# Cross attention: the normalised probabilities split into two f16 parts in SBUF and turned by one transposing DMA a chunk, the keys by another, and an f32 product with the fused output weights

## The reference, cut to what matters

```python
# image_embeds = ctx_1024, latents = layernorm(x after layer 0)
x = layer_norm(image_embeds, ln1_g, ln1_b)
l = layer_norm(latents, ln2_g, ln2_b)
q = l @ Wq
kv = jnp.concatenate([x, l], axis=1) @ Wkv      # 64 context rows + 64 latent rows a sequence
k, v = jnp.split(kv, 2, axis=-1)                # 16 heads of 64 channels
w = softmax(einsum('bhqd,bhkd->bhqk', q * scale, k * scale))
out = einsum('bhqk,bhkd->bhqd', w, v)
return out.reshape(B, S_lat, INNER) @ Wo        # added to x
```

## Time and profile before

| what | us |
| --- | --- |
| median of 3 runs | 1600.94 |
| profiled execution, its own time | 1598.53 |
| its span, first to last instruction | 1596.6 |
| PE busy | 1392.2 (87%) |
| DVE busy | 1355.3 (85%) |
| ACT busy | 1280.3 (80%) |
| POOL busy | 1079.0 (68%) |

### The profile page before, as it was taken

How to read it: one execution, slowest core, us unless ns; L and a number is a source line. 1 busy time by engine, 2 the same in 40 slices (tenths; PEclk the granted TensorE clock), 3 DMA queues, 4 the chain that set the end, 5 groups by cost and what they waited for, 6 DMA issues and landing times. The chain is left out here.

```text
span 1596.6 us, 53031 instructions
## 1 busy us (share of the span) xinstructions
PE 1392.2 (87%) x17084; PEld 1186.1 (74%) x17084; DVE 1355.3 (85%) x3979; ACT 1280.3 (80%) x3930; POOL 1079.0 (68%) x1524
## 2 busy tenths in 40 slices
PE   4779889974799999999999999999999719999970
PEld 3667777763688888888888888888888618888860
DVE  4479999995799999999999999999999628888877
ACT  1358888875799999999999999999999616666645
POOL 0367877763666577887788778877887555666650
PEclk7989999986899999999999999999999959999995
DMA  5445553400100000000000000000000013332209
GB/s 145 140 158 180 192 202 148 160 2 5 27 13 12 13 20 20 23 22 19 18 22 22 18 18 22 22 18 18 22 15 9 22 43 91 87 84 77 80 28 316
DMA packets 99738, 101.83 MB, mean 64 GB/s; under 512 B 15305, under 2 KB 81132, under 8 KB 99457
## 3 DMA queue, kind: packets, MB, share of 16 engines
q1 hardware_dynamic: 82496, 78.77, 15.4%
q0 software_dynamic: 8640, 16.93, 3.2%
q10 hardware_dynamic: 8448, 4.20, 0.9%
HBM read 39.40 MB, written 57.16 MB: 60 GB/s over the span
## 5 line engine op out<-in xcount | busy, mean ns | idle before, releaser
L1227 ACT ACTIVATE c_p<-bank,c_nmax 128x128 f32<-128x128 f32 x1024 | 368.9, 401 | 2.2 <-DVE c_nmax L1081 1.3
L1016 POOL TENSOR_TENSOR c_p<-c_p,c_rden 128x512 f32<-128x512 f32 x256 | 266.8, 1042 | 110.4 <-DVE c_rden L1091 106.0
L1227 ACT ACTIVATION_READ_ACCUMULATOR c_p<-bank,c_nmax 128x1 f32 x1024 | 244.2, 241 | 0.0
L1403 POOL DMA_INDIRECT moe_outputs<-e_y,e_to x142 | 152.9, 1077 | 93.3 <-DVE e_y L1434 58.6
L112 PE MATMUL bank<-c_kvT,qk_fused 128*128 128x128 f16 x1024 | 185.8, 220 | 10.8 <-ACT c_kvT L1206 10.4
L1081 DVE TENSOR_REDUCE c_nmax<-bank 128x4 f32<-128x512 f32 x256 | 173.4, 677 | 17.5 <-PE bank L114 14.3
L114 PE MATMUL bank<-c_kvT,qk_fused 128*128 128x128 f16 x1024 | 185.7, 220 | 0.0
L113 PE MATMUL bank<-c_kvT,qk_fused 128*128 128x128 f16 x1024 | 185.7, 220 | 0.0
L1473 ACT ACTIVATE e_h<-bank,moe_b 128x256 f32<-128x256 f32 x284 | 117.9, 466 | 65.7 <-PE bank L114 64.4
L1297 PE MATMUL bank<-const,c_p 128*128 128x128 f32 x1024 | 155.9, 275 | 3.6 <-DVE c_pT0rest L1102 1.7
L1059 POOL DMA_INDIRECT moe_slots<-r_rows,r_pos x128 | 131.6, 1028 | 34.9 <-issue 34.9
(11 more groups left out here) (324 smaller groups left out, 5921.0 us busy)
## 6 DMA issues: line engine op xcount, KB each, us to landing
moe_slots<-slot_fill SPq DMA_DIRECT2D x66, 520.0 KB, 5.6
e_rows<-moe_slots SPq DMA_DIRECT2D x71, 130.0 KB, 2.2
f_z<-moe_outputs SPq DMA_DIRECT2D x32, 256.0 KB, 4.9
x<-in_x SPq DMA_DIRECT2D x16, 256.0 KB, 3.2
a_ctx<-in_ctx SPq DMA_DIRECT2D x32, 128.0 KB, 3.4
moe_stage<-in_L_ffn_W SPq DMA_DIRECT2D x16, 256.0 KB, 3.1
c_rows<-in_ctx SPq DMA_DIRECT2D x128, 32.0 KB, 2.0
c_rows<-x SPq DMA_DIRECT2D x128, 32.0 KB, 1.8
```

Of the source, the lines that this page charges most:

```text
L1016: pool.tensor_tensor(pr[r % 4][:], pr[r % 4][:], rep(rden[r % 4][:], 2, P), ALU.mult).then_inc(m["pn"], 1)
L1227: last = act.activation(pr[r % 4][:, h, :], SB[r % 2][:, P * h:P * h + P], ACT.Exp, bias=nmax[r % 4][:, h:h + 1], accum_out=den[r % 4][:, ...
L1403: pool.indirect_dma_start(s.z, bass.IndirectOffsetOnAxis(ap=to[t % YBUF][:, h:h + 1], axis=0), ys[t % YBUF][:, h, :], None, bounds_check=2 ...
```

## The change

The probabilities are no longer transposed on the PE and then split. POOL now writes the product of exponentials and reciprocals as the high f16 part (`c_p_parts`, part 0); DVE forms the rest from the untouched exponentials with four `scalar_tensor_tensor` instructions of 128x128 (stage LOW, one chunk position after PN, both inputs and the output in SBUF); SP issues one transposing DMA for both parts (128 rows by 1024 f16), into one of four `c_pT` buffers. The keys are turned by a second transposing DMA a tile, into one of four `c_kvT` buffers, in place of PE transposes and an ACT copy. O is written once, in f32, by ACT, from two PSUM banks in turn. `s.vo` is kept in f32, and W is four f32 matmuls a chunk. Rows are loaded for two tiles at a time. The stages PT and KVT with their waits are gone, and `wait_rows` with them.

```diff
-                to = s.qk if n < 4 else s.vo
-                dve.wait_ge(pr_mh, n + 1)
-                dve.tensor_tensor(to[:, 1, heads, :], src, to[:, 0, heads, :], ALU.subtract).then_inc(pr_mc, 1)
+                if n < 4:
+                    dve.wait_ge(pr_mh, n + 1)
+                    dve.tensor_tensor(s.qk[:, 1, heads, :], src, s.qk[:, 0, heads, :], ALU.subtract).then_inc(pr_mc, 1)
+                else:
+                    dve.wait_ge(pr_m, n + 1)
+                    dve.tensor_copy(s.vo[:, heads, :], src).then_inc(pr_mc, 1)
...
-        kvt = [sb(f"c_kvT{n}", [P, 2, 4, 64], F16) for n in range(2)]
+        kvt = [sb(f"c_kvT{n}", [P, 2, 4, 64], F16) for n in range(4)]
         gs = [parts(f"c_g{n}", [P, 2, HEADS1, SEQ]) for n in range(2)]
         pr = [sb(f"c_p{n}", [P, 4, P]) for n in range(4)]
-        ptc = [parts(f"c_pT{n}", [P, 4 * P]) for n in range(2)]
-        os_ = [parts(f"c_o{n}", [P, HEADS1, P]) for n in range(2)]
+        pp = [sb(f"c_p_parts{n}", [P, 2, 4 * P], F16) for n in range(4)]
+        ptc = [sb(f"c_pT{n}", [P, 2, 4 * P], F16) for n in range(4)]
+        os_ = [sb(f"c_o{n}", [P, HEADS1, P]) for n in range(2)]
         norm_mul, norm_add = sb("c_norm_mul", [P, 2]), sb("c_norm_add", [P, 2])
...
-        AT_STATS, AT_RSTD, AT_KVN, AT_KV, AT_KVT, AT_G, AT_S, AT_PN, AT_PT, AT_O, AT_W, AT_X3 = 15, 13, 12, 11, 7, 6, 3, 2, 0, -1, -5, -9
+        AT_STATS, AT_RSTD, AT_KVN, AT_KV, AT_G, AT_S, AT_PN, AT_LOW, AT_O, AT_W, AT_X3 = 15, 13, 12, 11, 6, 3, 2, 1, -1, -5, -9
...
+            def load(n):
+                if n >= 2:
+                    sp.wait_ge(m["kvn"], 2 * n - 2)
                 for half in range(2):
                     rows = slice(64 * half, 64 * half + 64)
-                    sp.dma_start(cs[k][rows, 1 - half, :], cvw[1 - half, t, :, :]).then_inc(c_loaded[k], 16)
-                    sp.dma_start(cs[k][rows, half, :], s.xg(i)[rows, k, :]).then_inc(c_loaded[k], 16)
-            walk(sp, 0, TILES, 4, 4, TILES, step)
+                    to = cs[n % 2]
+                    sp.dma_start(to[rows, :, 1 - half, :], cvw[1 - half, 2 * n:2 * n + 2, :, :].rearrange("t s d -> s t d")).then_inc(c_loaded[n % 2], 16)
+                    sp.dma_start(to[rows, :, half, :], s.xg(n // 2)[rows, 2 * (n % 2):2 * (n % 2) + 2, :]).then_inc(c_loaded[n % 2], 16)
+
+            def turn_keys(v):
+                sp.wait_ge(m["kv"], v + 1)
+                if v >= 4:
+                    sp.wait_ge(m["s"], 4 * (v - 3))
+                sp.dma_start_transpose(kvt[v % 4][:].rearrange("p n a c -> p (n a c)").rearrange("p (b c) -> p b c", b=4),
+                                       kvs[v % 4][:].rearrange("p n b d -> p (n b d)")).then_inc(kvt_in[v % 4], 16)
+
+            def turn_weights(v):
+                sp.wait_ge(m["p_split"], v + 1)
+                if v >= 4:
+                    sp.wait_ge(m["o"], v - 3)
+                sp.dma_start_transpose(ptc[v % 4][:].rearrange("p a (b c) -> p (a b) c", b=4), pp[v % 4][:].rearrange("p a c -> p (a c)")).then_inc(pt_in[v % 4], 16)
+
+            load(0)
+            load(1)
+            for n in range(FIRST, CHUNKS):
+                if 0 <= n + AT_LOW < CHUNKS:
+                    turn_weights(n + AT_LOW)
+                if (n + 9) % 4 == 0 and 0 <= n + 9 < CHUNKS:
+                    turn_keys((n + 9) // 4)
+                if (n + 23) % 8 == 0 and 4 <= (n + 23) // 4 < TILES:
+                    load((n + 23) // 8)
...
-                    pool.tensor_tensor(pr[r % 4][:], pr[r % 4][:], rep(rden[r % 4][:], 2, P), ALU.mult).then_inc(m["pn"], 1)
+                    wait(pool, pt_in[r % 4], 16 * (4 * i + (k + AT_PN) // 4))
+                    pool.tensor_tensor(pp[r % 4][:, 0, :].rearrange("p (h c) -> p h c", h=4), pr[r % 4][:], rep(rden[r % 4][:], 2, P),
+                                       ALU.mult).then_inc(m["p_high"], 1)
...
+                if n := number(i, k, AT_LOW, CHUNKS):
+                    v, r = n
+                    dve.wait_ge(m["p_high"], v + 1)
+                    for h in range(4):
+                        cols = slice(P * h, P * h + P)
+                        last = dve.scalar_tensor_tensor(pp[r % 4][:, 1, cols], pr[r % 4][:, h, :], rden[r % 4][:, h:h + 1], pp[r % 4][:, 0, cols],
+                                                        ALU.mult, ALU.subtract)
+                    last.then_inc(m["p_split"], 1)
...
-                if n := number(i, k, AT_PT, CHUNKS):
-                    v, r = n
-                    hi, lo = ptc[r % 2]
-                    dve.wait_ge(m["pt_high"], v + 1)
-                    dve.tensor_tensor(lo[:], PT[:], hi[:], ALU.subtract).then_inc(m["pt_copied"], 1)
-                if n := number(i, k, AT_O, CHUNKS):
-                    v, r = n
-                    half, b = r % 2, r // 2 % 2
-                    hi, lo = [part[:, 8 * half:8 * half + 8, 64 * b:64 * b + 64] for part in os_[r // 4 % 2]]
-                    dve.wait_ge(m["o_high"], v + 1)
-                    dve.tensor_tensor(lo, OB[:].rearrange("p (h c) -> p h c", h=8), hi, ALU.subtract).then_inc(m["o_copied"], 1)
                 if t := tile(i, k, AT_STATS):
...
-                if t := tile(i, k, AT_KVT):
-                    v, r, _ = t
-                    act.wait_ge(m["kvt"], v + 1)
-                    wait(act, m["s"], 4 * (v - 1))
-                    act.activation(kvt[r % 2][:].rearrange("p n a c -> p (n a c)"), KVB[:, 0:512], ACT.Copy).then_inc(m["kvt_copied"], 1)
...
-                    act.activation(os_[r // 4 % 2][0][:, 8 * half:8 * half + 8, 64 * b:64 * b + 64],
-                                   OB[:].rearrange("p (h c) -> p h c", h=8), ACT.Copy).then_inc(m["o_high"], 1)
+                    act.activation(os_[r // 4 % 2][:, 8 * half:8 * half + 8, 64 * b:64 * b + 64],
+                                   OB[r % 2][:].rearrange("p (h c) -> p h c", h=8), ACT.Copy).then_inc(m["o_copied"], 1)
...
-                    wait(act, m["pt"], v - 3)
+                    wait(act, m["p_split"], v - 3)
...
-                        last = pe.transpose(PT[:, P * h:P * h + P], pr[r % 4][:, h, :], s.ident)
-                    last.then_inc(m["pt"], 1)
...
-                    pe.wait_ge(m["pt_copied"], v + 1)
-                    wait(pe, m["o_copied"], v)
-                    parts_product(pe, OB[:], [kvs[r // 4][:, part, r // 2 % 2, :] for part in range(2)], [part[:] for part in ptc[r % 2]]).then_inc(m["o"], 1)
+                    pe.wait_ge(pt_in[r % 4], 16 * (4 * i + (k + AT_O) // 4 + 1))
+                    wait(pe, m["o_copied"], v - 1)
+                    parts_product(pe, OB[r % 2][:], [kvs[r // 4][:, part, r // 2 % 2, :] for part in range(2)],
+                                  [ptc[r % 4][:, part, :] for part in range(2)]).then_inc(m["o"], 1)
...
-                        last = parts_product(pe, WB[:, 0:P], [part[:, h, :] for part in os_[r // 4 % 2]], [s.vo[:, part, h, :] for part in range(2)],
-                                             h == 0, h == HEADS1 - 1)
+                        last = pe.matmul(WB[:, 0:P], os_[r // 4 % 2][:, h, :], s.vo[:, h, :], start=h == 0, stop=h == HEADS1 - 1)
...
-        s.vo = sb("vo_fused", [P, 2, HEADS1, P], F16)
+        s.vo = sb("vo_fused", [P, HEADS1, P])
...
```

More of the change, by code:

```diff
@@ L223, in _ @@
                 heads = slice(8 * (n % 4 // 2) + n % 2, 8 * (n % 4 // 2) + n % 2 + 7, 2)
-                to = s.qk if n < 4 else s.vo
-                dve.wait_ge(pr_mh, n + 1)
-                dve.tensor_tensor(to[:, 1, heads, :], src, to[:, 0, heads, :], ALU.subtract).then_inc(pr_mc, 1)
+                if n < 4:
[4 more added lines that the diff above has]
+                    dve.tensor_copy(s.vo[:, heads, :], src).then_inc(pr_mc, 1)
         @block.scalar
         def _(act):
-            for n in range(8):
+            for n in range(4):
                 act.wait_ge(pr_m, n + 1)
                 src = s.pb[4 + n % 2][:].rearrange("p (k c) -> p k c", k=4)
-                heads = slice(8 * (n % 4 // 2) + n % 2, 8 * (n % 4 // 2) + n % 2 + 7, 2)
-                to = s.qk if n < 4 else s.vo
-                act.activation(to[:, 0, heads, :], src, ACT.Copy).then_inc(pr_mh, 1)
+                heads = slice(8 * (n // 2) + n % 2, 8 * (n // 2) + n % 2 + 7, 2)
+                act.activation(s.qk[:, 0, heads, :], src, ACT.Copy).then_inc(pr_mh, 1)
         @block.tensor
@@ L903, in cross_attention @@
     sem = s.sem
-    c_loaded = [sem(f"c_ctx_loaded{n}") for n in range(4)]
-    names = ("stats rstd kvn kv kvt kvt_copied g g_high g_copied s max exp rden pn pt pt_high pt_copied o o_high o_copied w x3")
+    c_loaded = [sem(f"c_ctx_loaded{n}") for n in range(2)]
+    kvt_in = [sem(f"c_kvt_in{n}") for n in range(4)]
+    pt_in = [sem(f"c_pt_in{n}") for n in range(4)]
+    names = "stats rstd kvn kv g g_high g_copied s max exp rden p_high p_split o o_copied w x3"
     m = {n: sem("c_" + n) for n in names.split()}
@@ L1122, in step @@
                     for n in range(2):
[L1123 removed]
```

(28 more changed lines are left out.)

30 lines of the change are left out of this document (6 added, 24 removed).

## The result

The kernel after takes 1797.5 us (median of 4 runs, 1790.0 to 1802.1) against 1600.9 (4 runs, 1597.2 to 1602.8): a ratio of 1.123 with a 95% interval of 1.118 to 1.127. It is slower, inside the range and 59 us under the forecast. The profiled execution took 1799.3 us. In two of the later sets of runs, those of e5 to e7 and of e12, every time is longer, the median of before too (1678.7 and 1678.4 us); what follows the last PN took 51 to 82 us more in their profiles than in that of before, for no known cause, so totals are compared by the ratio to before in the same set.

What follows compares the result with a forecast made beforehand. PE was taken to bound the kernel before, with ACT and DVE just behind. A pace of 4.3 us gave (4.3 - 3.305) x 256 = +255 us on 1598.5, 1853, and with 2.4 for the median 1856 us; range 1660 to 1980.

Steps and rivals of the forecast that it cites:

- The exclusion: Cross attention: DVE instructions with two SBUF inputs (LOW) and POOL's tensor instructions can't run together; pace 4.3 us, chance 0.55.
- DVE alone: DVE's work a chunk without any exclusion: 3.14 - 1.20 for two rests + 1.06 for LOW = 3.00 us.
- What the exclusion adds: In DVE's step: 1.00 us of PN inside LOW, at most 0.6 from POOL's other work; upper end 4.6, taken 4.3.
- the signs named beforehand: If right: LOW's four last some 2.3 us ending after PN, PE near 70%, PN's starts 4.3 us apart.
- The scatter doesn't hold two-input work: POOL's scatter leaves two-input DVE instructions alone: L1134 ran its 0.17 us inside it.
- PE and ACT: Work a chunk after the change: PE falls from 3.26 to 2.98 us, ACT to at most 2.6 us.
- PE sets the pace: Cross attention before the change: PE's 3.26 us a chunk sets the 3.305 us pace, ACT and DVE just behind.
- rival A: The SBUF pair costs little, PE and DVE bound the stage: 3.1 us a chunk, 1549 us; chance 0.16.
- B: The transposing DMA bounds the stage: 4.9 us a chunk, +408, about 2009 us; chance 0.07.
- C: PE's clock falls for a fifth of the stage, adding 82 us: 1938 us; chance 0.08.
- D: DVE keeps the SBUF pair through LOW's four and POOL waits: 3.7 us a chunk, 1702 us; chance 0.12.
- the DMA's price: Transposing DMA of the probabilities, 256 KB a chunk: 3 to 5 us from issue to landing, no wait at the taken pace.

Runs made afterwards that it cites:

- e5: The kernel before with only the f32 output product and one-part O, transposes still on PE: ratio 1.014 to before, 3.437 us a chunk.
- e7: The changed kernel with the high part copied by ACT, PN in f32 in place and one DVE subtraction ahead of the reciprocal: ratio 1.045 to before.
- e12: The changed kernel with probabilities in one f16 part, no LOW instructions, and DVE's remaining wait for PN moved to a chunk earlier: ratio 0.960 to before.
- e1: The changed kernel with one of LOW's two SBUF inputs read from G's PSUM bank, so the true rest is left out: 1593.6 us, ratio 0.997.
- e2: The changed kernel with PN normalizing two of the four heads, the other high parts left zero: 1685.9 us, ratio 1.054 to before.
- e3_order: The changed kernel with LOW moved ahead of the reciprocal that releases the next PN, same result: 1669.1 us, ratio 1.043 to before.
- e8: The kernel before with only the keys turned by a transposing DMA, in place of PE transposes and an ACT copy: ratio 1.003 to before.
- e10: The changed kernel with LOW reading PSUM and two of its four instructions left out: ratio 0.973 to before, 3.160 us a chunk.
- e6: The changed kernel with each transposing DMA of the probabilities issued twice, first into a spare tile: 1921.9 us, ratio 1.144 to before.
- e9: The kernel of e1 with two PSUM banks for W and one for O: ratio 0.994 to before, 3.297 us a chunk.

## Why the prediction was right, and where its numbers were off

**The mechanism held.** The exclusion was forecast from the earlier trace rows, at the place where LOW stands behind the reciprocal. e1 removes it alone and takes back the whole loss; e2 gives it a dose. The Trainium skill, page "SBUF — State Buffer", section "Who interferes with whom", has the same rule, with two limits: two SBUF inputs exclude only a GpSimd (POOL) instruction which reads SBUF, and an instruction with at most one SBUF input does not contend. The trace agrees: PN and the keys' instructions read SBUF, and with one input in PSUM (e1) LOW took 1.10 us beside them.

**DVE alone.** 3.00 us forecast; in e1, where it stands alone, 91.68% of 3.298 is 3.02. In after the part outside LOW is 3.98 - 2.13 = 1.85, forecast 1.94.

**What the exclusion adds: the mis-sized term.** The prediction put 1.00 inside LOW and up to 0.6 on top of 3.00, and took 4.3, that is 1.3 in all. LOW's four grew from 1.10 to 2.13, by 1.03; with DVE's idle 0.11 the pace is 4.09. Both pieces were taken too large. PN doesn't cost its 1.05 but about 0.8 (1.89 against 1.09 in the groups shown); it starts while LOW's first still runs. POOL's other work adds the remaining 0.2, not 0.3 to 0.6: a group that also meets one of the keys' instructions lasts some 2.4 us, as here in after, 0.5 more than 1.89 however many of them run beside it. Timelines of DVE, then POOL:

```profile
834.76 2.44 DVE L1126 SCALAR_TENSOR_TENSOR c_p_parts<-c_p,c_rden,c_p_parts 128x128 f16<-128x128 f32 x4
```

```profile
836.01 0.77 POOL L1065 TENSOR_TENSOR c_kv<-c_kv,ln_b 128x256 f32<-128x256 f32 x1
836.93 0.80 POOL L1067 TENSOR_TENSOR c_kv_parts<-c_kv,c_kv_parts 128x256 f16<-128x256 f32 x1
```

With the measured pace the sum gives (4.093 - 3.305) x 256 = +202 where +255 was forecast; +201 was measured. Of the signs named beforehand PE's share came out at 77%, not near 70, for the same reason: the pace is shorter than 4.3.

**"The scatter doesn't hold two-input work" held, but a PN that waits behind the scatter does.** In the timeline of after, LOW's second and third run beside the scatter of 825.87 at about 0.3 us, but the fourth, begun at 826.54, needs 1.72 us. The scatter ends at 827.01 and PN comes only at 827.05, so something held the fourth before PN's record begins. The view of that line and stretch:

```profile
L1126 DVE SCALAR_TENSOR_TENSOR c_p_parts<-c_p,c_rden,c_p_parts x4: 315/338/1717, 825.8 to 826.5; 128x128 f16<-128x128 f32 x4
```

e3_order tells the two apart, since its reciprocal stands behind LOW, so that no PN is released yet when LOW runs. There all four run at their usual length inside a scatter, the last of them from 893.2 to 893.5 (line of LOW, cut to this group, then POOL's timeline):

```profile
L1122 DVE SCALAR_TENSOR_TENSOR c_p_parts<-c_p,c_rden,c_p_parts x4: 346/346/351, 892.4 to 893.2; 128x128 f16<-128x128 f32 x4
```

```profile
892.50 1.10 POOL L1088 DMA_INDIRECT moe_slots<-r_rows,r_pos  x1 [0.17 <-issue]
```

Over the whole of e3_order 74 instructions of LOW began more than 0.5 us into a scatter, and none took over 0.351 us. In after, 43 did: the 18 that began when the reciprocal for the next PN had ended took 1.57 to 1.78 us, the 25 that began before its end 0.31 to 0.32. So the scatter holds nothing by itself; a PN that is released and next on POOL takes effect before its record begins. By what means is open.

**PE and ACT.** PE was forecast at 2.98 busy; it shows 3.15 in after and 3.07 in e1. W's f32 matmul leaves two records, 275 ns by median, eight of them in 1.05 us, as expected. ACT: 2.68 for "at most 2.6". Neither matters to after's pace.

**"PE sets the pace" of before was too simple.** It decided rival A: 3.0 us of work, so 3.1 of pace. e1 shows 3.30 in just that case, with the clock at full. e8 takes work off PE and nothing comes; e10 takes 0.53 off DVE and 0.14 comes. PE waits for DVE's G rest and X3, DVE for PE's scores, and the step is longer than either sum by 0.2 to 0.3 us. How that ring is composed is open. So even with no exclusion the change would have brought 0.3% (e1), not 3%. Rival A's gain of 0.2 us a chunk was lost in this ring before the exclusion took anything.

**B, C and D.** B is out by e6 and e1. Of C a little is there: the granted clock averages 0.96 over nearly all of after's stage, part of it at 1.2 GHz in place of 2.4, where before has 1.00. Windows of after, the stage and then two stretches of 16 chunks:

```profile
425.00:1465.00 1040.00, 816.44 (x8983) 692.71 (x8980) 1000.37 (x2632) 674.95 (x2602) 675.74 (x881) 0.96 0.44 86
1000.00:1066.00 66.00, 50.34 (x577) 42.53 (x576) 64.24 (x172) 42.90 (x167) 44.89 (x59) 1.00 0.44 87
1270.00:1338.00 68.00, 55.38 (x577) 47.04 (x577) 64.56 (x172) 43.27 (x166) 44.97 (x60) 0.90 0.43 85
```

At 1.00 the pace is 4.14 us, at 0.90 it is 4.26, with DVE busy for 95 instead of 97%. That the clock is the cause of these 0.12 us, about a sixth of the loss in such a stretch, was not tested.

D (3.7 us) would want LOW at 1.13 us; it took 2.13. As for the DMA's price, one lands 3.1 us after its issue, within the 3 to 5 us taken. The 10.5 us for eight blocks in a row, an estimate from the Trainium skill's figure for one block (page "VectorE: DVE Perf Modes", section on the three transpose paths), does not hold here: e1 ran such a transfer every 3.30 us.

## What to carry to other kernels

Before work moves to DVE, ask whether the new instruction reads two tensors in SBUF, and which instruction of POOL its place in the order releases; the price was about 0.8 us for POOL's instruction of 1.05, once each time, and reading one input from PSUM or changing the order shows it at once. Where all engines stand at nine tenths, the largest busy sum is a lower bound of the pace and no more: take a little off one engine and see whether the step shortens, before counting on the next sum. A wait that a view names is only worth removing if what stands behind it is early; twice here (e9, e12) another took its place.

## What the runs showed of the hardware

A transposing DMA of 256 KB (eight blocks of 128x128 f16) occupied SP for 1.23 us and landed 3.1 us after its issue, about as long as the plain 256 KB of x took the earlier trace rows. Its line in after:

```profile
L1025 SPq DMA_TRANSPOSE c_pT<-c_p_parts x256: 1231/1232/2718, 420.0 to 1463.9; - x128
...
DMA to landing us min/median/max: 3.0/3.1/5.0
```

Its packets are small: the second one of e6 brings 270,336 packets for 256 transfers, 1,056 each, some 250 bytes a packet (queues of e6_twice, then of after):

```profile
q1 hardware_dynamic: 655936, 221.44, 54.7%
```

```profile
q1 hardware_dynamic: 385600, 154.30, 36.4%
```

PN writing f16 took 1.05 us where f32 took 1.04, so the output's type made no difference that counts. Back-to-back instructions of DVE do not keep POOL out: in after POOL's PN got in between the first and the second of four that had no wait between them, and in the group of 834.76 the keys' instruction of 836.01 between the second and the third, which then took 0.81 us. Where POOL's has begun first, DVE's is held from its start: the first of e3's four at 826.09, 0.06 us behind the keys' instruction, took 0.76 us.
